# A four-layer graph network on one core: layer 1's node points made by one group after the other

## The reference

```
h = lorentz_linear(x, W, b)      # linear, then a "time" entry and a rescaling of the other 63
q, k = lorentz_linear(h, Wq), lorentz_linear(h, Wk)
time = sigmoid(h[:, :1]) * exp(scale) + 1.1
s = (time * time - 1) / sum(xn * xn);  point = [time, xn * sqrt(s)]
att = adj * sigmoid((2 + 2 * (qm @ k.T)) / att_scale + att_bias)     # qm is q with its time negated
support = att @ h;  out = support / sqrt(|inner(support)|)
```

## Time and profile before

| | us |
|---|---|
| median of 3 runs (lowest, highest) | 1091.84 (1090.72, 1092.6) |
| profiled execution | 1090.43 |
| its span, first to last instruction | 1088.7 |
| TensorE busy in it | 1036.7 (95%) |
| VectorE busy | 862.8 (79%) |
| ScalarE busy | 767.5 (71%) |
| GpSimd busy | 270.7 (25%) |
| mean granted TensorE clock | 0.987 |

### The profile page before, as it was taken

One profiled execution on the slowest core, in us unless ns is written; L12 is line 12 of the kernel. 1 busy time (PEld: TensorE's weight loads), 2 busy tenths in 40 slices (PEclk: granted clock), 3 DMA queues, 4 the chain that ended last, 5 costly groups with the idle time before them and its releaser, 6 DMA issues.

```text
span 1088.7 us, 14887 instructions
## 1 busy us (share of the span) xinstructions
PE 1036.7 (95%) x5430; PEld 448.2 (41%) x5430; DVE 862.8 (79%) x1013; ACT 767.5 (71%) x807; POOL 270.7 (25%) x140
## 2 busy tenths in 40 slices
PE   7999999999789999999979999999999998989998
PEld 2333333336633333334324443444554554436544
DVE  7999989996766666697669987887789887898781
ACT  5555455553556656676688899988888888997682
POOL 1089500000010000003015364434343433440010
PEclk9999999999989999999999999999999999999999
DMA  9989989980048888778754445555455545446451
GB/s 353 396 343 423 393 322 346 359 331 30 2 154 274 280 290 280 247 274 288 245 180 136 135 135 175 177 172 193 155 168 181 170 140 174 136 140 208 140 173 40
DMA packets 96341, 238.32 MB, mean 219 GB/s; under 512 B 16400, under 2 KB 45072, under 8 KB 79888
## 3 DMA queue, kind: packets, MB, share of 16 engines
q1 hardware_dynamic: 87056, 220.62, 58.3%
q10 hardware_dynamic: 9216, 16.78, 4.0%
HBM read 219.55 MB, written 17.83 MB: 218 GB/s over the span
## 4 chain that ended last, share of the span: by engine, by line
PE 74%; DVE 12%; ACT 9%; issue 4%; DMA 1%; SPq 0%; DVEq 0%; ACTq 0%
PE PS L563 51%; PE PS L737 5%; PE PS L738 5%; PE PS L870 4%; PE PS L839 4%; ACT work L1224 2%; ACT work L1232 2%; DVE work L1969 2%; DVE work L1957 1%; ACT work L1235 1%; DVE ring L1975 1%; DVE work L1963 1%; ACT work L1218 1%; PE PS L575 1%; ACT work L1155 1%
## 5 line engine op out<-in xcount | busy, mean ns | idle before, releaser
L1637 DVE TENSOR_TENSOR work<-work,ring 128x1024 f32<-128x1024 f32 x128 | 151.2, 1223 | 76.8 <-ACT work L1155 76.7
L1155 ACT ACTIVATE work<-PS,att_sc 128x1024 f32<-128x1024 f32 x128 | 147.7, 1202 | 85.7 <-PE PS L738 78.4
L1090 ACT ACTIVATE work<-PS 128x1024 uint8<-128x1024 f32 x128 | 124.0, 1020 | 107.6 <-PE PS L563 107.6
L563 PE MATMUL PS<-ring,work 128*65 128x256 f32 (+1 forms) x600 | 191.8, 467 | 4.1 <-DVE work L1996 4.0
L541 POOL TENSOR_TENSOR ring<-work,ring 128x1024 f32<-128x1024 f32 x57 | 135.9, 2384 | 236.6 <-DVE work L1969 236.5
L563 PE MATMUL PS<-work 128*64 128x512 f32 (+2 forms) x800 | 153.6, 526 | 1.1 <-ACT work L1218 1.0
L1963 DVE SCALAR_TENSOR_TENSOR work<-PS,work 128x1024 f32<-128x1024 f32 x72 | 88.0, 1223 | 53.8 <-PE PS L563 45.3
L563 PEld LDWEIGHTS PS<-ring,work 128*65 128x65 f32 x600 | 80.8, 139 | 91.5 <-issue 66.0
L737 PE MATMUL PS<-work 128*128 128x512 f16 x256 | 98.9, 386 | 2.0 <-DVE work L1444 1.3
L1224 ACT ACTIVATE work<-work 128x1024 f32<-128x1024 f32 x72 | 76.0, 1055 | 34.8 <-DVE work L1957 34.7
L738 PE MATMUL PS<-work 128*128 128x512 f16 x256 | 98.2, 384 | 0.0
(11 more groups left out here) (267 smaller groups left out, 1479.9 us busy)
## 6 DMA issues: line engine op xcount, KB each, us to landing
ring<-in_adj_t SPq DMA_DIRECT2D x96, 1024.0 KB, 5.3
ring<-in_adj_t SPq DMA_DIRECT2D x104, 512.0 KB, 3.8
work<-in_adj_t SPq DMA_DIRECT2D x32, 1024.0 KB, 8.3
codes<-work ACTq DMA_DIRECT2D x64, 256.0 KB, 7.4
ring<-codes SPq DMA_DIRECT2D x64, 256.0 KB, 3.7
H<-in_adj_t SPq DMA_DIRECT2D x24, 512.0 KB, 3.9
X<-in_x SPq DMA_DIRECT2D x2, 256.0 KB, 4.5
X<-in_x SPq DMA_DIRECT2D x1, 512.0 KB, 9.9
```

Source lines behind the costliest of these rows:

```text
L563: return mm(out_ap, lhsT, rhs, start=starts, stop=True, skip_group_check=True)
L1090: nc.scalar.activation(made[:, k, u * UNIT:(u + 1) * UNIT], PS[:, (4 + 2 * u) * BANK:(6 + 2 * u) * BANK], ACT.Relu).then_inc(sem("codes_ma ...
L1155: nc.scalar.activation(att[:, u, :], PS[:, (4 + 2 * u) * BANK:(6 + 2 * u) * BANK], ACT.Sigmoid, bias=att_sc[:, 2:3], scale=att_sc[:, 1:2]) ...
L1637: V.tensor_tensor(prob[:, m % 4, :], att[:, u, :], ring[:, s % RING, u * UNIT:(u + 1) * UNIT], ALU.mult)\
```

## The change

Layer 1's points are made by group instead of in pairs.

- Group 0's layer-1 norm is made inside the second half of layer 0, in steps T+8 to T+15, on VectorE (sums_l1, centre_l1, spread_l1, feats_l1: the old norm for one group) and ScalarE; it is written over `cen`, not H, which layer 0 still reads. The first eight of the loop's steps are written out for this.
- TensorE flips `cen` for group 0 before the last to_nodes and makes its h linear before the degrees. The degrees are in one piece (32 tiles, a filler behind every other), with 4 fillers behind them and 8 more further on (28 in all, 48 before).
- h, q and k of group 0 go ahead of those of group 1. The small operations are the same ones, in lorentz_sum, lorentz_ratio, lorentz_factor and lorentz_point, called for a list of (tag, group) points. The k points have statistics and a square buffer of their own (`cen`).
- Scores start when q and k of group 0 are folded. Of group 1, q's z is copied from PSUM to H (zq_out), since scores need its banks, and its points, f16 parts and folds stand in layer 1's steps 1 to 14: key point at step 1, its high part at 2, low at 3, fold at 5, copy at 6; q point at 7, high part at 8, fold of it at 10, copy at 11; fold of q's low part at 13, copy at 14. z of k for group 1 stays in PSUM banks 2 and 3 until step 1.
- GpSimd's low parts wait only for the high parts.

The diff, cut to its core (new helpers that hold the old operations for one group are left out):

```diff
-        HBk = nodes(slot(7))
+        HBk = [work[:, k * UNIT:(k + 1) * UNIT].rearrange("p (t c) -> p t c", t=TG) for k in (14, 6)]
...
-        BEFORE = {"h": 0, "q": G, "k": 2 * G}
+        POINTS = (("h", 0), ("h", 1), ("q", 0), ("k", 0), ("q", 1), ("k", 1))
+        TAGS = {"h": (st[1], st[2], st[3], st[4], st[6], sqr), "q": (st[1], st[2], st[3], st[4], st[6], sqr),
+                "k": (st[7], st[8], st[5], st[9], st[0], cen)}
+        def nth(tag, g):
+            return POINTS.index((tag, g)) + 1
...
-                pool.wait_ge(sem("q_point" if g == 0 else "khl_out"), G if g == 0 else 1)
...
+            pe.wait_ge(sem("feats_ready_l1"), 1)
+            flip(cen, 0, 0).then_inc(sem("flipped"), 1)
             pe.wait_ge(sem("sums_out0_v"), 1)
             to_nodes(wbd["l0"][:, :], UNIT, 2, 0).then_inc(sem("z0_ready"), 1)
             pe.wait_ge(sem("codes_made"), 4 * T)
+            pe.wait_ge(sem("flip_out"), 1)
+            linear(wbd["l1"][:, :], 1, 0, 4).then_inc(sem("lin_h"), 1)
             pe.wait_ge(sem("deg_added"), 2 * T)
-            def degrees(g, bank, spare, idle):
-                for t in range(g * TG, (g + 1) * TG):
+            def degrees(bank, spare):
+                for t in range(T):
                     ins = mm(PS[:, bank * BANK + t:bank * BANK + t + 1], TB[:, t * P:(t + 1) * P], ones[:, :], start=True, stop=True)
-                    if t - g * TG >= idle:
+                    if t % 2 == 0:
                         keep_at_work(spare)
                 ins.then_inc(sem("deg_summed"), 1)
-            degrees(0, 7, 5, 0)
-            for _ in range(22):
-                keep_at_work(5)
-            for g in range(G):
-                pe.wait_ge(sem("feats_ready_l1"), g + 1)
-                flip(H, g, 0).then_inc(sem("flipped"), 1)
+            degrees(7, 6)
+            for _ in range(4):
+                keep_at_work(6)
+            pe.wait_ge(sem("feats_ready_l1"), 2)
+            flip(H, 1, 0).then_inc(sem("flipped"), 1)
+            pe.wait_ge(sem("feats1_ready"), 1)
+            flip(HL, 0, 0).then_inc(sem("flipped"), 1)
             pe.wait_ge(sem("deg_out"), 1)
-            for g in range(G):
-                pe.wait_ge(sem("flip_out"), g + 1)
-                linear(wbd["l1"][:, :], 1, g, 4).then_inc(sem("lin_h"), 1)
-            degrees(1, 3, 2, 6)
-            for g in range(G):
-                pe.wait_ge(sem("feats1_ready"), g + 1)
-                if g:
-                    pe.wait_ge(sem("deg_out"), 2)
-                flip(HL, g, 0).then_inc(sem("flipped"), 1)
-            for g in range(G):
-                pe.wait_ge(sem("flip_out"), G + g + 1)
-                linear(wbd["q"][:, :], 2, g, 4).then_inc(sem("lin_q"), 1)
-            for g in range(G):
-                linear(wbd["k"][:, :], 3, g, 0).then_inc(sem("lin_k"), 1)
+            pe.wait_ge(sem("flip_out"), 2)
+            linear(wbd["l1"][:, :], 1, 1, 4).then_inc(sem("lin_h"), 1)
+            pe.wait_ge(sem("flip_out"), 3)
+            linear(wbd["q"][:, :], 2, 0, 4).then_inc(sem("lin_q"), 1)
+            linear(wbd["k"][:, :], 3, 0, 0).then_inc(sem("lin_k"), 1)
+            for _ in range(8):
+                keep_at_work(2)
+            pe.wait_ge(sem("feats1_ready"), 2)
+            flip(HL, 1, 0).then_inc(sem("flipped"), 1)
+            pe.wait_ge(sem("flip_out"), 4)
+            linear(wbd["q"][:, :], 2, 1, 4).then_inc(sem("lin_q"), 1)
+            linear(wbd["k"][:, :], 3, 1, 0).then_inc(sem("lin_k"), 1)
...
-            for g in range(G):
+            def fold_high(g, dst):
                 pe.wait_ge(sem("q_high"), g + 1)
-                fold(Q2, 0, g, 4 + 2 * g).then_inc(sem("qhh_ready"), 1)
+                fold(Q2, 0, g, dst).then_inc(sem("qhh_ready"), 1)
             def fold_low(g, dst):
                 pe.wait_ge(sem("q_low"), g + 1)
                 fold(Q2, 1, g, dst).then_inc(sem("qll_ready"), 1)
+            fold_high(0, 4)
...
-                    pe.wait_ge(sem("qhh_out"), 2)
+                    pe.wait_ge(sem("zq_out"), 1)
...
-                if s == 0:
+                if s == 5:
                     fold_both(1)
-                if s == 4:
+                if s == 10:
                     pe.wait_ge(sem("khl_out"), 2)
+                    fold_high(1, 2)
+                if s == 13:
+                    pe.wait_ge(sem("qhh_out"), 2)
                     fold_low(1, 2)
...
+                if h:
+                    for k in range(MADE):
+                        make_code(1, T + MADE + k, k, MADE + k, (T // MADE + 1) * 16)
+                        if k == 1:
+                            one("ln_sq", grp(sqr, 0), grp(cen, 0), ACT.Square, ("ln_centred", G + 2))
+                        if k == 4:
+                            power_of("ln_sd", st[2], st[1], -0.5, "ln_var", G + 1, (0,))
+                with act.Fori(1 + h, T // MADE) as it:
...
+            flipped_out(0, 0)
+            lorentz_squares("h", 4, 0)
+            one("ln_sq", grp(sqr, 1), grp(cen, 1), ACT.Square, ("ln_centred", G + 3))
+            power_of("ln_sd", st[2], st[1], -0.5, "ln_var", G + 2, (1,))
+            lorentz_roots(("h", 0))
+            flipped_out(0, 1)
+            flipped_out(1, 0)
+            lorentz_squares("h", 4, 1)
+            lorentz_squares("q", 4, 0)
+            lorentz_roots(("h", 1))
+            lorentz_squares("k", 0, 0)
+            flipped_out(1, 1)
+            lorentz_roots(("q", 0), ("k", 0))
+            lorentz_squares("q", 4, 1)
+            lorentz_squares("k", 0, 1)
+            high("q", HBq(0), Q2(0), 0)
+            high("k", HBk[0], grp(K2, 0), 0)
             folded_out("qhh_out", q_hh, 0, 4, "qhh_ready")
+            one("zq_out", HBq(1), z_of(4, 1), ACT.Copy, ("lin_q", 2))
             folded_out("qll_out_a", q_ll, 0, 4, "qll_ready")
+            lorentz_roots(("q", 1), ("k", 1))
...
+                if s == 2:
+                    high("k", HBk[1], grp(K2, 1), 1)
+                if s == 8:
+                    high("q", HBq(1), Q2(1), 1)
+                if s == 11:
+                    folded_out("qhh_out", q_hh, 1, 2, "qhh_ready")
...
+                    for k in range(RING0):
+                        mask0(T + RING0 + k, k, (T // RING0 + 2) * 16, False)
+                        degree0(1, T + RING0 + k - 2, (k - 2) % RING0)
+                        if k == 0:
+                            sums_l1(0)
+                        if k == 1:
+                            centre_l1(0)
+                        if k == 4:
+                            spread_l1(0)
+                        if k == 7:
+                            feats_l1(0, cen)
+                with dve.Fori(1 + h, T // RING0) as it:
...
-            norm_stats(1, range(G))
+            sums_l1(1)
+            centre_l1(1)
...
+            lorentz_sum("h", 0)
+            spread_l1(1)
+            dve.wait_ge(sem("time_consts"), 2)
+            lorentz_ratio(("h", 0))
             dve.wait_ge(sem("agg0_done"), 2 * T)
+            feats_l1(1, H)
+            feature_point(0)
+            dve.wait_ge(sem("deg_summed"), 1)
+            V.tensor_scalar(deg[:, :], PS[:, 7 * BANK:7 * BANK + T], 1e-8, None, ALU.max).then_inc(sem("deg_out"), 1)
             link(V.reciprocal(att_sc[:, 0:1], scal[:, 4:5]))
             link(V.tensor_scalar(att_sc[:, 0:1], att_sc[:, 0:1], 2.0, None, ALU.mult))
             link(V.tensor_scalar(att_sc[:, 1:2], att_sc[:, 0:1], top[:, 1:2], top[:, 2:3], ALU.mult, ALU.mult))
             V.tensor_scalar(att_sc[:, 2:3], att_sc[:, 0:1], scal[:, 3:4], None, ALU.add).then_inc(sem("att_scale_ready"), 1)
+            lorentz_sum("h", 1)
+            lorentz_ratio(("h", 1))
+            lorentz_sum("q", 0)
+            feature_point(1)
+            lorentz_sum("k", 0)
+            lorentz_ratio(("q", 0), ("k", 0))
             for k in range(MADE):
                 dve.wait_ge(sem(f"codes_stored{k}"), 2 * T // MADE * 16)
+            lorentz_factor(("q", 0), ("k", 0))
+            query_point(0, z_of(4, 0))
+            key_point(1, 0)
+            lorentz_sum("q", 1)
             def key_low(g):
                 dve.wait_ge(sem("k_high"), g + 1)
+                V.tensor_tensor(grp(K2, g)[:, :, 1, :], HBk[g], grp(K2, g)[:, :, 0, :], ALU.subtract)\
                  .then_inc(sem("k_low"), 1)
             def keys_out(g):
                 copy_out("khl_out", k_hl[:, g * HALF:(g + 1) * HALF], banks(2 * g, 2 * g + 2).bitcast(F16), ("khl_ready", g + 1))
             key_low(0)
+            lorentz_sum("k", 1)
+            lorentz_ratio(("q", 1), ("k", 1))
             keys_out(0)
...
-            key_low(1)
             def product(s, u):
                 m = 2 * s + u
-                if m == 1:
-                    dve.wait_ge(sem("k_low"), 2)
...
                 if s == 1:
+                    lorentz_factor(("k", 1))
+                    key_point(0, 1)
+                if s == 3:
+                    key_low(1)
+                if s == 6:
                     keys_out(1)
-                if s == 4:
```

(24 more changed lines are left out.)

153 lines of the change are left out of this document (72 added, 81 removed).

## The result

The changed kernel takes **1082.26 us** (median of 12 runs, 1078.2 to 1088.71) where the kernel before takes 1092.42 (12 runs, 1088.31 to 1095.08): ratio 0.992, 95% interval 0.9897 to 0.9943 (the two medians alone give 0.9907). I had predicted 1081.5, range 1078.0 to 1086.8. The profiled execution of after took 1079.82, 10.61 less than that of before.

What follows compares the result with a forecast made beforehand. The passage between layers 0 and 1 was taken as a sum of latencies, the layers beside it as TensorE-bound. Passage -11.3 and layer 1 +0.9 gave -10.4 us, from 1091.84 to 1081.4, given as 1081.5, range 1078.0 to 1086.8.

Steps and rivals of the forecast that it cites:

- Norm in layer 0, price 0: Layer 0, steps T+8 to T+15: 5.9 us of added VectorE work is covered by mask lead, 2.8 us left.
- TensorE's head, +0.9: Start of the passage: group 0's flip ahead of the last to-nodes matmuls delays the update of X by 0.9 us.
- the path that changes over to TensorE by 2.4 us: Passage, at group 1's flip: TensorE's degrees and fillers end at 265.6, after VectorE's features, so TensorE is 2.4 us later.
- Passage: Between layer 0 and the first score: first score at 293.5 instead of 304.77, 11.3 us earlier.
- Layer 1, +0.9: Inside layer 1: three folds added at steps 5, 10, 13, one key fold removed before step 1; net +0.9 us.
- rival 3: Layer 1, steps 1 to 14: no slack, every overrun and hand-over lands on the path; 1083.5 to 1086.5; chance 0.12.
- The rule that splitting costs 2 us: Small operations of the passage: by fixed instruction cost, splitting six ratios and factors by group loses about 2 us; not added.
- low from about 288 to 299: End of the passage and first scores: the stretch in which TensorE's clock was forecast to be low.
- 32 degree matmuls ... 0.565 a pair ... = 9.0: Passage: TensorE's degrees, every other with a filler, priced at 0.565 us a pair, 9.0 us from 255.75 to 264.75.
- rival 1: Passage: the clock falls earlier, q1 and k1 linears at 1.2 GHz take 4.4 us more; 1086.7; chance 0.10.
- Rival 2: End of passage and first scores: the clock holds, folds save 1.7 us, scores and what follows 2.8; 1077; chance 0.07.

Runs made afterwards that it cites:

- extra reductions: Changed kernel plus five unread 128x1024 VectorE reductions (5.9 us) in steps T+10 to T+14 of layer 0; one run, 1083.77 us, TensorE waits 2.1.
- clock_kept: Changed kernel with 22 filler matmuls in TensorE's three waits at the end of the passage; 1080.87 us, ratio 0.9878.
- tail_first: Changed kernel with group 1's points, parts, folds and copies put back ahead of the first score; 1099.85 us, ratio 1.0052.
- low_in_turn: Changed kernel with GpSimd's first subtraction (queries) made to wait until VectorE's (keys) is done; 1085.94 us.
- next_order: degrees_spread with ScalarE's and VectorE's queues reordered for the first score and the last five degrees behind the q high fold; 1076.52 us, ratio 0.9838.
- fewer_fillers: Changed kernel with a filler behind every fourth degree matmul instead of every second, and without the four behind them; 1085.33 us, ratio 0.9913.
- filler_each: Changed kernel with a filler behind each of the 32 degree matmuls and the four behind the last one gone; 1082.61 us, ratio 0.9908.
- degrees_spread: Changed kernel with degrees split 21, 6 and 5 into TensorE's waits, a filler behind each, and other gaps filled as in clock_kept; 1077.82 us, ratio 0.9866.
- spread_again: The kernel of degrees_spread measured once more, beside the changed kernel run again; 1078.32 us, ratio 0.985 against the kernel before.

## Why the prediction was right

The forecast took the mechanism that the trace shows. Its times, with the 1.88 us of the later start added, against those of the trace:

| | predicted | in the trace |
|---|---|---|
| flip of H, group 1 | 267.5 | 267.44 |
| linear h, group 1 | 269.7 | 269.68 |
| flip HL, group 1 | 279.7 | 278.82 |
| end of the key square, group 1 | 286.3 | 286.69 |
| fold of q high | 287.4 | 287.76 |
| first score | 295.4 | 295.92 |

- *Norm in layer 0, price 0:* right. No wait of TensorE, and a mask T+16 that is written at 191.5 and wanted at 194.9: 3.3 of lead, 2.8 had been predicted. The extra reductions bear it out. The two rows:

```profile
190.31 1.22 DVE L1541 TENSOR_SCALAR work<-ring 128x2048 bf16<-128x2048 f32 x1
```

```profile
194.85 0.60 PE L568 MATMUL PS<-work,tri_rest 128*128 128x512 bf16 x2
```

- *TensorE's head, +0.9, and the path that changes over to TensorE by 2.4 us:* right. VectorE had the features at 265.30 and TensorE was free at 267.44. Moving the degrees away gave the 2.1 at the flip, and 1.2 of it at the first score.
- *Passage:* -10.73 where -11.3 was predicted, by small release delays.
- *Layer 1, +0.9:* it came to +0.11. The three folds in the steps cost 1.76 more than the one that was there, as counted. The mis-sized part is the key fold that is gone from in front of step 1. The sum took 0.9 off for it, but in the trace of before it ran at the low clock and took 1.71 (308.15 to 309.86):

```profile
308.15 1.91 PE L715 MATMUL PS<-identh,work 128*128 128x128 f16 x16
309.86 0.63 PE L737 MATMUL PS<-work 128*128 128x512 f16 x1
...
313.92 0.39 PE L737 MATMUL PS<-work 128*128 128x512 f16 x1
```

  Step 2 starts 9.15 us after the first score there and 7.50 in the changed kernel: 1.65 sooner, nearly all of it this fold. The clock adds little to that: it came back some 3.0 us after the first score instead of 5.8, in both near the start of step 1's scores, and the eight scores of step 0 take 3.25 us instead of 3.38. The gap of 0.38 at 300.58, a wait for ScalarE's sigmoid, is all that the trace has of rival 3.
- *The rule that splitting costs 2 us:* the sum holds without it. That the split work lay under TensorE's degrees and linears fits the rows above; no run tests it alone.
- *The clock:* "low from about 288 to 299" is what the profiled run shows. What I missed is that the same code has other places to fall. The step that failed is **"32 degree matmuls ... 0.565 a pair ... = 9.0"**: a price at the full clock (9.1 us in the profiled run) for a stretch that runs in part at half speed in some executions, for 2.8 to 6.1 us more. 4 of the 12 runs lie above my range. I had asked under rival 1 what the clock does in the gaps, and had not asked it of a stretch without gaps.
- *Rival 2* gave 1077 for a clock that holds. The clock in clock_kept held and gave 1080.87, since behind the faster folds and scores ScalarE's and VectorE's queues ended last: 2.1 of the 4.5 us.

## What to carry to other kernels

When a node-wise passage between two full stages is a chain of latencies, split it by group, and hide the head of one group in the stage before and the tail of the other in the stage after. Both were needed here: with either one undone the gain was gone (in tail_first even less the 6.1 us that its clock cost). In such a passage order every engine's queue by what the first instruction of the next stage needs, and lay work that TensorE owes anyway (the degrees) into its waits. With a filler behind each degree they kept the clock at 1.00 here.

## What the runs showed of the hardware

**VectorE and GpSimd exclude each other in two-input operations.** In the changed kernel VectorE's subtraction, issued at 288.69, ends 1.08 us after GpSimd's is over (289.98), as if it had only started then. At 332.52, by the rows below, two products take 3.60 us instead of 2.36, while GpSimd's subtraction, issued at 330.91 during an earlier product, takes 3.00 instead of 2.12 and ends at 333.91: whoever comes second waits.

```profile
330.91 3.00 POOL L505 TENSOR_TENSOR H<-H 128x1024 f16<-128x1024 f32 x1 [40.93 <-ACT H L1053]
```

```profile
332.52 3.60 DVE L1717 TENSOR_TENSOR work<-work,ring 128x1024 f32<-128x1024 f32 x2 [0.61 <-ACT work L1175]
```

The Trainium skill ("SBUF — State Buffer", SBUF: two separate sides) describes the two engines' common port pair as a lock held for a whole instruction; low_in_turn and next_order agree, with 1.23 and 1.21 us once the two don't meet. I hadn't put this into the prediction's sum; with the low clock after it, it cost nothing on the path, but with the clock kept up to 0.8 (in clock_kept the keys are folded at 294.11 and copied from 294.90).

**The clock can fall while TensorE is fully busy in the profile.** In tail_first, fewer_fillers and low_in_turn it went from 1.00 to 0.50 in the middle of one-column matmuls, with 5.00 of 5.00 us busy. That a stretch was busy throughout did not mean that the clock would hold. With a filler behind every single one it held in the degrees of all four profiled runs that had this (filler_each, degrees_spread, spread_again, next_order); with one behind every second it held in most and fell in two. The Trainium skill ("TensorE: Matmul & The Clock Gate", Part 1) ties the clock to how busy TensorE has been; the busy time of these rows gives no sign of the fall. What made it fall in one execution and not in another is not shown.

What stays open: no run of the changed kernel itself above 1085 was caught in a profile. That its clock fell in the degrees there is argued from low_in_turn and tail_first, which have the same code up to that place, and from the kernels without the fall, whose spread is 1.6 to 2.9 us.
